# A two-layer window-attention and clustering network on one core: other TensorE work between scores and flips, and three unread products at each strip's end

## The chip, the cores and the metric

One Trainium2 chip, one core. The metric is the time of one execution on the device in microseconds (us): the median over runs. Three runs of the kernel before gave 10057.81, 10078.72 and 10090.93 us.

## What is computed

The input is x, 2 x 96 x 256 x 256 in fp32; the output has its shape. Two layers follow one another, each a mixing part and a feed-forward network.

Layer 0 is cut into four 128 x 128 quadrants per image (8 in all). In a quadrant, with a halo of 2, windows of 8 x 8 queries attend to 12 x 12 keys, with 6 heads of 16 and a relative position term:

```
xn   = (x - mean_c) * rsqrt(var_c + 1e-6)
S    = q k^T + rel_w + rel_h          # 64 x 144 per window and head
x1   = x + proj(softmax(S) v)
x2   = x1 + W2 relu(W1 q(ln(x1)) + b1) + b2    # fp8 weights and operands, fp16 sums
```

Layer 1 pools features of a quadrant into 4 centres per head (4 heads of 24), gives every point to its nearest centre by cosine similarity (the winner alone, with a sigmoid weight), gathers the points' values by centre, and mixes them back to the points: `xc = x2 + proj(sim * agg)`. Its feed-forward network is like that of layer 0.

## The kernel before

**Tiling.** The 8 quadrants have 16 strips of 8 rows each, N = 128 strips. A strip is 32 windows, 16 to the left and 16 to the right in parity, worked on as TILES = 8 pairs p; a pair fills 128 partitions with 2 windows of 64 queries.

**Stages.** Strips run as a software pipeline. In step n, `attend` does the attention of strip n, the preparation of strip n + 1 (mean, variance, normalisation, keys, queries, values: `ahead`), the feed-forward network of strip n - 1 (`b1`), pooling of n - 2 (`b2`), from step 18 on (LAG_B) the features and similarities of the quadrant before (`on.b`), from step 34 on (LAG_C) mixing and the second feed-forward network (`on.c1`, `c2`, `c3`). This gives three stages: steps 0 to 17, 18 to 33, 34 to 127. Behind them, 34 `drain` steps finish layer 1 for the last quadrants. Between quadrants, `edge` works out the centres.

**Order of the work.** Each engine has its own program, written out by hand; a Signal is a semaphore with a count per step, and `at(n, k)` is the value at which the k-th of step n is done. The order in a program is thus the order on the engine: nothing is reordered by a planner. PE's program is written out for 16 strips in a loop over quadrants; DVE's loop body in stage 3 holds two strips.

**A strip on PE** (`attend`, L624 to 841). scores(0); flip_z(0) of strip n - 1; make_values(1); then for each p: scores(p+1) into both banks of `scores_x` (L627, waits until DVE has shifted pair p), flip(p, 0) and flip(p, 1) (L646, transposes of the shifted scores into `flipped`, wait for the shift of p), weigh(p-1) (L669, probabilities times values, waits for the exponentials of p - 1), and then other work, which differs by p: mean, flip_z(1), output_c at 0; mean, flip_features, hidden at 1; hidden, variance, features at 2; hidden, variance, flip_zc, make_values(2) at 3; make_values(3), flip_sims and output at 4; pool, flip_heads, spread, hidden_c at 5; project, spread, hidden_c at 6; hidden_c and mix at 7. The tail (L816 to 841) is make_keys 0 and 1, weigh(7), then make_queries 0 to 5 with make_keys 2 and 3, flip_heads(1), make_main, project(1) and make_rest between them, and gather.

**PSUM.** Eight banks: `work` (bank0, bank1) for mean, spread, values, queries, features, flip_zc and mix; `scores_x` (two) for scores, and at the strip's end for make_keys, whose results ACT stores (k_stored); `flipped` (two) for the flips, hidden layers, outputs and the first values; `pv`; and `misc` for small transposes and projections.

**A strip on DVE** (L1468 to 1576). For each p: maximum of the scores (L1496), two subtractions (L1500, L1504), and then other work: stats_c (L1729) and rsqrt_c (L1740, nine small operations in a row, each waiting for the one before) at p = 0; centre_x at 1 and 2; output_c at 1; hidden (L1611, bias and relu of layer 0) at 2, 3, 4; normalise_c (L1748) at 2; compare at 3; variance, a Newton step and lengths at 4; normalise(0) (L1471) and cosine at 5; normalise_x, output, hidden_c at 6 and 7. Then mix (L1722), next_stats (L1626), normalise(1), ffn_stats, pool_stats, ffn_normalise(0), hidden_c, best_of (L1688), residual(1), ffn_stats, ffn_normalise(1), and add_gathered (L1716, waits for PE's gather). The next strip's first maximum follows.

**A strip on ACT** (L1133 to 1230). For each p: two exponentials (L1147, L1150), then evacuations, squares and quantisations for the work that PE has done in that pair; in the tail, the stores of keys (L1107), queries (L1113) and values.

**POOL** masks values, gathers windows and normalises the stream; **SP** issues all transfers. Neither program changes.

```
def make_keys(n, c):
    ...
    mm(score[c % 2][0:C, 0:CH], wk[0:PROW, :], xn_flat[0:PROW, c * CH:(c + 1) * CH],
       start=True, stop=True).then_inc(k_ready.sem, 1)
```

Here CH is 396, a quarter of a strip's 1584 columns.

## Time and profile before

| | |
|---|---|
| median of three runs | 10078.72 us (10057.81 to 10090.93) |
| the profiled execution | 10158.83 us, its span 10157.0 us |
| mean granted TensorE clock | 0.860 |
| PE busy | 9070.3 us (89%), 177778 instructions |
| PE weight loads busy | 7381.3 us (73%) |
| DVE busy | 7288.7 us (72%), 24125 |
| ACT busy | 5171.8 us (51%), 10122 |
| POOL busy | 2170.7 us (21%), 4356 |
| DMA | 509 MB, 50 GB/s in the mean |

A busy PE is not a PE at its peak: the time of a matmul in the profile includes its passage through the array, and at the lower clock the same instruction takes about twice as long. The granted clock is therefore read beside every busy share. What a wait costs is read from the chain of waits and from the timeline of the stage, for an engine that waits off the chain loses nothing. The names in the rows are those of tensors without buffer numbers: `flipped` stands for both of its banks, `bank` for `work`, `later` for the buffers of layer 1 (xc, xn2b, xn2_t, feat_sq), `rz` for rs_c_chain, `z` for z8, `h` for h16 and h8.

### The profile page before, as it was taken

How to read it: one execution, taken by the hardware profiler on the slowest of the kernel's cores; microseconds unless marked ns; L12 is line 12 of the kernel's file. 1: busy time of each engine (PE TensorE's matmuls, PEld its weight loads, DVE VectorE, ACT ScalarE, POOL GpSimd, SP SyncE). 2: the span in 40 equal slices, each digit the busy share in tenths (PEclk: the TensorE clock that was granted, in tenths of full speed). 3: DMA queues.
4: the chain of work that ended last, by engine and by line, in shares of the span. 5: the costliest groups of instructions: out<-in, count | busy, mean ns of one | idle time of the engine just before them, and what ended most of it. 6: DMA issues, size and time to landing. Idle time of an engine off the chain costs nothing.

```text
span 10157.0 us, 445903 instructions
## 1 busy us (share of the span) xinstructions
PE 9070.3 (89%) x177778; PEld 7381.3 (73%) x177778; DVE 7288.7 (72%) x24125; ACT 5171.8 (51%) x10122; POOL 2170.7 (21%) x4356
## 2 busy tenths in 40 slices
PE   8999999999998999989999999989989999997666
PEld 6777778777777777777777777777777777776554
DVE  5777777777777777777777777777777777776555
ACT  4555444445555555555555555555555555554445
POOL 2333222222222222222222222222222222221000
PEclk9999998998898888888888888888888888897555
DMA  2111111112121211212111111112112112121111
GB/s 60 44 47 45 48 48 48 48 51 51 51 54 50 55 50 50 55 49 51 51 51 50 50 52 50 50 50 55 51 50 55 47 50 53 52 53 44 43 45 47
DMA packets 191702, 509.43 MB, mean 50 GB/s; under 512 B 33214, under 2 KB 66686, under 8 KB 189694
## 3 DMA queue, kind: packets, MB, share of 16 engines
q1 hardware_dynamic: 189918, 482.96, 17.9%
q8 instruction: 1447, 23.71, 1.0%
q14 instruction: 337, 2.76, 0.1%
HBM read 244.54 MB, written 160.43 MB: 40 GB/s over the span
## 4 chain that ended last, share of the span: by engine, by line
PE 70%; DVE 18%; issue 7%; ACT 4%; DVEq 0%; SPq 0%; ACTq 0%; DMA 0%; POOL 0%; POOLq 0%
PE scores_x L639 9%; PE flipped L661 8%; PE scores_x L580 4%; PE pv L689 4%; PE bank L609 4%; PE bank L546 3%; PE misc L555 3%; PE bank L927 3%; PE bank L598 3%; PE pv L683 3%; PE bank L900 3%; PE bank L616 2%; PE pv L883 2%; DVE maxes L1496 2%; PE misc L718 2%
## 5 line engine op out<-in xcount | busy, mean ns | idle before, releaser
L1931 POOL TENSOR_TENSOR vrest<-vstage,vmask 96x384 f32<-96x384 f32 x512 | 432.0, 844 | 5560.4 <-ACT vstage L1125 5560.2
L1496 DVE TENSOR_REDUCE maxes<-scores_x 128x6 f32<-128x864 f32 x1024 | 1078.2, 1053 | 573.3 <-PE scores_x L639 465.6
L639 PE MATMUL scores_x<-keys,queries 64*64 64x144 f32 x24576 | 1171.5, 328 | 297.2 <-DVE shifted L1504 283.2
L639 PEld LDWEIGHTS scores_x<-keys,queries 64*64 64x64 f32 x24576 | 855.2, 152 | 457.4 <-issue 408.1
L1147 ACT ACTIVATE probs<-flipped 128x384 f32<-128x384 f32 x1024 | 501.4, 490 | 1314.2 <-PE flipped L661 1313.7
L661 PE MATMUL flipped<-ident,shifted 128*128 128x128 f32 x6144 | 1034.5, 310 | 61.5 <-ACT h16c L1298 46.5
L661 PEld LDWEIGHTS flipped<-ident,shifted 128*128 128x128 f32 x6144 | 750.0, 156 | 346.9 <-issue 222.8
L601 PE MATMUL bank<-xn,wq 97*32 97x64 f32 x24576 | 946.8, 233 | 59.4 <-issue 59.0
L1504 DVE TENSOR_TENSOR shifted<-scores_x,maxes 128x768 f32<-128x768 f32 x1024 | 969.8, 947 | 0.2 <-issue 0.2
L598 PEld LDWEIGHTS bank<-xt,wq 97*32 97x32 f32 x24576 | 806.2, 119 | 205.1 <-issue 179.9
L598 PE MATMUL bank<-xt,wq 97*32 97x64 f32 x24576 | 929.0, 234 | 29.0 <-issue 27.8
L1113 ACT ACTIVATE queries<-bank 128x512 f32<-128x512 f32 x768 | 458.6, 597 | 835.4 <-PE bank L601 835.4
L601 PEld LDWEIGHTS bank<-xn,wq 97*32 97x32 f32 x24576 | 821.5, 117 | 43.0 <-issue 42.4
L1944 POOL TENSOR_SCALAR xn<-x,mr 128x96 f32<-128x96 f32 x1024 | 690.3, 686 | 42.3 <-DVE mr L1404 42.3
L689 PE MATMUL pv<-vmain,probs 128*32 128x17 f32 x49152 | 643.6, 189 | 3.5 <-issue 3.5
L689 PEld LDWEIGHTS pv<-vmain,probs 128*32 128x32 f32 x49152 | 638.6, 116 | 2.5 <-issue 2.4
L1150 ACT ACTIVATE probs<-flipped 128x512 f32<-128x512 f32 x1024 | 611.0, 597 | 55.5 <-PE flipped L664 54.4
L1904 POOL COPY xt<-xn 97x512 f32<-97x512 f32 x256 | 291.0, 1167 | 1493.2 <-DVE xn L1464 1493.2
L1613 DVE TENSOR_SCALAR h<-h,b1q 128x512 f16<-128x512 f16 x768 | 261.8, 351 | 450.4 <-ACT h L1240 409.6
L609 PE MATMUL bank<-wv,win_xn 97*128 97x96 f32 x3072 | 497.0, 313 | 96.3 <-ACT z8ct L1293 96.1
L580 PE MATMUL scores_x<-xn,wk 97*96 97x396 f32 x1024 | 564.4, 665 | 1.1 <-DVE xn L1464 0.7
L1298 ACT ACTIVATE h16c<-flipped 128x512 f16<-128x512 f32 x768 | 421.4, 591 | 281.2 <-PE flipped L945 281.2
(180 smaller groups left out, 19648.2 us busy)
## 6 DMA issues: line engine op xcount, KB each, us to landing
x_in<-x_dram SPq DMA_DIRECT2D x128, 594.0 KB
keys<-kst SPq DMA_DIRECT2D x768, 99.0 KB
xn_kept<-xn SPq DMA_DIRECT2D x128, 388.0 KB, 3.9
later<-xn_kept SPq DMA_DIRECT2D x128, 388.0 KB, 3.4
x_tok<-tok_dram SPq DMA_DIRECT2D x128, 384.0 KB, 3.5
x_kept<-x SPq DMA_DIRECT2D x128, 384.0 KB, 2.4
later<-x_kept SPq DMA_DIRECT2D x128, 384.0 KB, 4.7
out_dram<-later SPq DMA_DIRECT2D x128, 384.0 KB, 2.3
```

The costliest lines, as they stand in the source:

```text
L580: mm(score[c % 2][0:C, 0:CH], wk[0:PROW, :], xn_flat[0:PROW, c * CH:(c + 1) * CH], start=True, stop=True).then_inc(k_ready.sem, 1)
L598: mm(dst[64 * e:64 * e + 32, :, :, j], wq[0:PROW, p * WS + j, 2 * g + e, :], xt[0:PROW, p, j, :, :], start=True, stop=True, skip_group_che ...
L601: last = mm(dst[64 * e + 32:64 * e + 64, :, j, :], wq[0:PROW, 2 * WS + j, 2 * g + e, :], rows[:, j], start=True, stop=True, skip_group_che ...
L609: last = mm(dst[0][:, j * C:(j + 1) * C], win_xn[:, 4 * i + j, 0:MAIN], wv[0:PROW, :], start=True, stop=True)
L639: last = mm(score[e][64 * j:64 * j + 64, g * NKEY:(g + 1) * NKEY], queries[64 * e:64 * e + 64, g, w, :], keys[64 * e:64 * e + 64, g, :, WS ...
L661: last = nc.tensor.transpose(flipped[:, e, g * 128:(g + 1) * 128], shifted[:, p % 2, e * NG + g, :], ident[:, :])
L689: last = mm(pv[tok_, at + i * VC:at + (i + 1) * VC], probs[:, p % 2, i, tok_], vmain[:, 2 * p + part // 2, i, :], start=False, stop=True, ...
L1147: run(probs[:, p % 2, 0:NG, :].rearrange("p i n -> p (i n)"), flipped[:, 0, 0:NG * 128], ACT.Exp).then_inc(exp_ready.sem, 1)
L1150: run(probs[:, p % 2, NG:NH + 1, :].rearrange("p i n -> p (i n)"), flipped[:, 1, :], ACT.Exp).then_inc(exp_ready.sem, 1)
L1496: V.tensor_reduce(maxes[:, p % 2, :, :], sc, AX.X, ALU.max).then_inc(max_ready.sem, 1)
L1504: V.tensor_tensor(shifted[:, p % 2, :, :].rearrange("p (e g) k -> p e g k", e=2), sc[:, :, :, 0:MAIN], maxes[:, p % 2, :, :, None].to_broa ...
L1944: last = P.tensor_scalar(xn2[:, t, 0:C], x2[:, t, :], mr[:, t, 0:1], mr[:, t, 1:2], ALU.subtract, ALU.mult)
```

## The change

PE's program: in each pair, part of the other work is now done between scores(p+1) and the flips of p, and part of it goes to another pair. keep_busy is new: three products with the operands of make_keys into the score banks, with no signal; nothing reads what they write. mix goes from p = 7 to behind weigh(7). ACT's program follows PE's order. DVE's: rsqrt_c goes from p = 0 to 1, output_c from 1 to 2, normalise_c from 2 to 3, hidden from 2, 3, 4 to 3, 4, 5, normalise(0) behind cosine, normalise_x(0), (1) from 6 to 7, hidden_c from 6 and 7 to 7 alone. The first hunks of the diff are the PE program with its new function, the others ACT's and DVE's; lines with only "..." leave out unchanged or removed code.

```diff
@@ -580,6 +580,12 @@
+            def keep_busy(n, i):
+
+                pe.wait_ge(k_stored.sem, k_stored.at(n, 4))
+                mm(score[i % 2][0:C, 0:CH], wk[0:PROW, :], xn_flat[0:PROW, i * CH:(i + 1) * CH],
+                   start=True, stop=True)
+
@@ -726,97 +732,106 @@
                 for p in range(TILES):
                     if p + 1 < TILES:
                         scores(p + 1)
+                    if p == 0 and ahead:
+                        pe.wait_ge(v_stored.sem, v_stored.at(n, 4))
+                        mean(n + 1, 0)
+                        mean(n + 1, 1)
+                    if p == 1 and ahead:
+                        mean(n + 1, 2)
+                        mean(n + 1, 3)
+                    if p == 2 and on.b:
+                        for u in range(2):
+                            if ahead:
+                                pe.wait_ge(centred.sem, centred.at(n + 1, 3 + u))
+                            pe.wait_ge(v_stored.sem, v_stored.at(n, 4))
+                            features(n, u)
+                    if p == 3 and ahead:
+                        variance(n + 1, 2, on)
+                        variance(n + 1, 3, on)
+                    if p == 4:
+                        pe.wait_ge(v_stored.sem, v_stored.at(n, 4))
+                        if ahead:
+                            pe.wait_ge(centred.sem, centred.at(n + 1, 4))
+                        if on.c2:
+                            pe.wait_ge(zct_ready.sem, zct_ready.at(n, 2))
+                        elif on.b:
+                            pe.wait_ge(fsq_ready.sem, fsq_ready.at(n, 2))
+                            pe.wait_ge(dots_ready.sem, dots_ready.at(n, 2))
+                        make_values(n, 2, work)
+                    if p == 5:
+                        pe.wait_ge(v_stored.sem, v_stored.at(n, 6))
+                        make_values(n, 3, work)
+                    if p == 6:
+                        if ahead:
+                            spread(n + 1, 0)
+                            spread(n + 1, 1)
+                        flip_heads(0)
+                    if p == 7:
+                        if ahead:
+                            spread(n + 1, 2)
+                            spread(n + 1, 3)
+                        project(0)
                     flip(p, 0)
                     flip(p, 1)
                     if p >= 1:
                         weigh(p - 1)
                     if p == 0:
...
                         if b1:
                             flip_z(n - 1, 1)
                         if on.c3:
                             pe.wait_ge(exp_ready.sem, exp_ready.at(n, 2))
                             output_c(n, 0)
                             output_c(n, 1)
...
+                    if p == 1 and on.b:
+                        if b1:
+                            pe.wait_ge(zt_ready.sem, zt_ready.at(n - 1, 2))
+                        flip_features(n, 0, k % 2)
+                    if p == 2 and ahead:
+                        if b1:
+                            pe.wait_ge(zt_ready.sem, zt_ready.at(n - 1, 2))
+                        variance(n + 1, 0, on)
+                        variance(n + 1, 1, on)
+                    if p == 3 and on.c2:
+                        pe.wait_ge(fsq_ready.sem, fsq_ready.at(n, 2))
+                        pe.wait_ge(dots_ready.sem, dots_ready.at(n, 2))
+                        flip_zc(n, 0)
+                        flip_zc(n, 1)
+                    if p == 4 and on.c1:
                         if ahead:
...
+                            pe.wait_ge(newton_x.sem, newton_x.at(n + 1, 1))
+                        flip_sims(n, 0, on)
+                    if p == 5:
+                        if b2:
+                            pool(n - 2)
+                        if on.c1:
+                            flip_sims(n, 1, on)
                     if b1 and p in (1, 2, 3):
                         pe.wait_ge(exp_ready.sem, exp_ready.at(n, 2 * p + 2))
                         hidden(n - 1, 2 * p - 2)
                         hidden(n - 1, 2 * p - 1)
                     if p == 1 and on.b:
                         flip_features(n, 1, k % 2)
...
+                    if b1 and p == 4:
+                        pe.wait_ge(exp_ready.sem, exp_ready.at(n, 10))
+                        output(n - 1, 0)
+                        output(n - 1, 1)
                     if on.c2 and p in (5, 6, 7):
                         pe.wait_ge(exp_ready.sem, exp_ready.at(n, 2 * p + 2))
                         hidden_c(n, 2 * p - 10)
                         hidden_c(n, 2 * p - 9)
...
                 if ahead:
                     make_keys(n + 1, 0)
                     make_keys(n + 1, 1)
                 weigh(TILES - 1)
+                if on.c1:
+                    for u in range(2):
+                        if ahead:
+                            pe.wait_ge(normed.sem, normed.at(n + 1, 4 - u))
+                        pe.wait_ge(v_stored.sem, v_stored.at(n, 8))
+                        mix(n, u)
                 if ahead:
                     make_queries(n + 1, 0, on)
                     make_keys(n + 1, 2)
@@ -829,13 +844,16 @@
                         pe.wait_ge(hc_evac.sem, hc_evac.at(n, 5))
                     make_main(n + 1, 0, fill)
                     make_queries(n + 1, 3)
+                    keep_busy(n + 1, 0)
                 project(1)
                 if ahead:
                     make_queries(n + 1, 4)
+                    keep_busy(n + 1, 1)
                     make_queries(n + 1, 5)
                     if on.c2:
                         pe.wait_ge(hc_evac.sem, hc_evac.at(n, 6))
                     make_rest(n + 1, 0, fill)
+                    keep_busy(n + 1, 2)
                 if on.b:
                     pe.wait_ge(heads_ready.sem, heads_ready.at(n, 2))
                     gather(n, k % 2)
@@ -1141,6 +1159,22 @@
+                    if p == 1 and ahead:
+                        square(n + 1, 0)
+                        square(n + 1, 1)
+                    if p == 2:
+                        if ahead:
+                            square(n + 1, 2)
+                            square(n + 1, 3)
+                        if on.b:
+                            square_features(n, 0)
+                            square_features(n, 1)
+                    if p == 4:
+                        store_values(n, 2, work)
+                    if p == 5:
+                        store_values(n, 3, work)
+                    if p == 6:
+                        heads(0)
@@ -1156,9 +1190,6 @@
-                        if ahead:
-                            square(n + 1, 0)
-                            square(n + 1, 1)
@@ -1166,18 +1197,11 @@
-                    if p == 2:
-                        if b1:
-                            hidden(n - 1, 2)
-                            hidden(n - 1, 3)
-                            quantise(n - 1, 0)
-                            quantise(n - 1, 1)
-                        if ahead:
-                            square(n + 1, 2)
-                            square(n + 1, 3)
-                        if on.b:
-                            square_features(n, 0)
-                            square_features(n, 1)
+                    if p == 2 and b1:
+                        hidden(n - 1, 2)
+                        hidden(n - 1, 3)
+                        quantise(n - 1, 0)
+                        quantise(n - 1, 1)
@@ -1187,21 +1211,16 @@
-                        store_values(n, 2, work)
+                        if on.c1:
+                            store_sims(n, 0)
-                        store_values(n, 3, work)
-                        if on.c1:
-                            store_sims(n, 0)
-                        if b1:
-                        if on.c1:
-                            store_sims(n, 1)
-                    if p == 5:
-                        heads(0)
+                    if p == 5 and on.c1:
+                        store_sims(n, 1)
@@ -1507,21 +1526,23 @@
-                        rsqrt_c(n)
-                    if p == 1 and on.c3:
+                    if p == 1 and on.c2:
+                        rsqrt_c(n)
+                    if b1 and p in (3, 4, 5):
+                        hidden(n - 1, 2 * p - 6)
+                        hidden(n - 1, 2 * p - 5)
+                    if p == 2 and on.c3:
-                    if b1 and p in (2, 3, 4):
-                        hidden(n - 1, 2 * p - 4)
-                        hidden(n - 1, 2 * p - 3)
-                    if p == 2 and on.c2:
-                        normalise_c(n, 1 - par)
-                    if p == 3 and on.b:
-                        compare(n, 0)
-                        compare(n, 1)
+                    if p == 3:
+                        if on.b:
+                            compare(n, 0)
+                            compare(n, 1)
+                        if on.c2:
+                            normalise_c(n, 1 - par)
@@ -1533,13 +1554,10 @@
-                        normalise(0)
+                        normalise(0)
-                        if ahead:
-                            normalise_x(n + 1, 0)
-                            normalise_x(n + 1, 1)
@@ -1548,12 +1566,18 @@
+                            normalise_x(n + 1, 0)
+                            normalise_x(n + 1, 1)
+                        if on.c2:
+                            hidden_c(n, 0)
+                            hidden_c(n, 1)
+                        if ahead:
-                    if on.c2 and p in (6, 7):
-                        hidden_c(n, 2 * p - 12)
-                        hidden_c(n, 2 * p - 11)
+                        if on.c2:
+                            hidden_c(n, 2)
+                            hidden_c(n, 3)
```

## Rows read from the trace of the kernel before

**Rows 1.** The page: granted TensorE clock in 40 slices; the chain's shares by engine.

```profile
PEclk9999998998898888888888888888888888897555
...
PE 70%; DVE 18%; issue 7%; ACT 4%; DVEq 0%; SPq 0%; ACTq 0%; DMA 0%; POOL 0%; POOLq 0%
```

**Rows 2.** Windows by stage: us, busy us of each engine (instructions), granted clock, DMA share, GB/s.

```profile
74.00:1075.00 1001.00, 947.48 (x23085) 780.16 (x23084) 707.21 (x2127) 513.14 (x993) 298.73 (x606) 0.98 0.18 46
1075.00:2101.00 1026.00, 973.61 (x21232) 814.26 (x21233) 744.31 (x2292) 499.88 (x976) 270.39 (x545) 0.91 0.19 48
2101.00:9297.00 7196.00, 6554.08 (x130040) 5347.04 (x130041) 5341.34 (x17620) 3761.60 (x7407) 1588.80 (x3174) 0.88 0.20 51
```

**Rows 3.** Waits of PE in stage 3: who waited for whom: us in total, times, longest.

```profile
PE scores_x L639 <- DVE shifted L1504: 261.4, 119, 5.7
PE bank L609 <- ACT z8ct L1293: 96.1, 93, 1.1
PE flipped L945 <- ACT probs L1150: 90.1, 93, 1.0
PE flipped L661 <- ACT h16c L1298: 46.5, 93, 0.6
```

**Rows 4.** Windows of one strip of stage 3, cut where the granted clock changes.

```profile
7095.60:7099.10 3.50, 0.43 (x14) 0.45 (x17) 3.33 (x10) 0.54 (x2) 0.00 (x0) 1.00 0.15 54
7099.10:7102.50 3.40, 3.40 (x71) 2.66 (x66) 3.20 (x8) 1.21 (x3) 0.00 (x0) 0.50 0.06 23
...
7119.60:7123.00 3.40, 3.40 (x35) 2.84 (x35) 3.06 (x14) 1.79 (x4) 0.84 (x1) 0.50 0.00 0
...
7143.50:7150.30 6.80, 6.80 (x128) 4.70 (x130) 3.53 (x15) 1.77 (x4) 3.60 (x14) 0.50 0.01 2
```

**Rows 5.** Timeline of DVE, the same strip: start, us, line, what, idle before.

```profile
7093.11 0.18 DVE L1742 TENSOR_SCALAR rz<-mv_z 128x8 f32<-128x8 f32 x1
...
7093.56 1.65 DVE L1387 TENSOR_TENSOR rz<-rz 128x8 f32<-128x8 f32 x1
...
7096.33 1.05 DVE L1496 TENSOR_REDUCE maxes<-scores_x 128x6 f32<-128x864 f32 x1
...
7119.04 0.84 DVE L1613 TENSOR_SCALAR h<-h,b1q 128x512 f16<-128x512 f16 x2 [2.98 <-ACT h L1240]
...
7122.80 1.05 DVE L1496 TENSOR_REDUCE maxes<-scores_x 128x6 f32<-128x864 f32 x1
```

**Rows 6.** Chain of waits, the same strip: start, us on the chain, engine and line.

```profile
7098.69 1.37 PE scores_x L639 x24
...
7120.99 1.65 PE scores_x L639 x24
...
7124.46 1.06 PE bank L609 x8
...
7128.10 0.90 PE scores_x L639 x24
...
7142.34 2.59 PE bank L927 x16
7144.93 2.88 PE scores_x L580 x4
...
7150.56 0.84 PE scores_x L580 x2
```

**Rows 7.** Timeline of ACT, the same strip.

```profile
7124.27 1.14 ACT L1246 ACTIVATE h<-h 128x512 fp8e5<-128x512 f16 x2
```

**Rows 8.** Timeline of DVE, end of this strip and start of the next.

```profile
7149.13 0.16 DVE L1475 COPY pool_parts<-pv 97x2 f32 x1 [2.32 <-PE pv L689]
...
7166.33 0.17 DVE L1719 TENSOR_TENSOR gathered<-gathered,pv 97x16 f32<-97x16 f32 x1 [2.76 <-PE pv L908]
7169.41 1.06 DVE L1496 TENSOR_REDUCE maxes<-scores_x 128x6 f32<-128x864 f32 x1 [2.91 <-issue]
```

**Rows 9.** Window of PE's transposes and one-column products in the same strip.

```profile
7130.60:7133.70 3.10, 3.10 (x38) 2.68 (x37) 1.50 (x3) 0.69 (x2) 0.00 (x0) 1.00 0.28 106
```

More of the change, by code:

```diff
@@ L781, in attend @@
-                    if p == 4:
-                        pe.wait_ge(v_stored.sem, v_stored.at(n, 6))
-                        make_values(n, 3, work)
-                        if on.c1:
-                            if ahead:
-                                pe.wait_ge(newton_x.sem, newton_x.at(n + 1, 1))
-                            flip_sims(n, 0, on)
-                        if b1:
-                            pe.wait_ge(exp_ready.sem, exp_ready.at(n, 10))
-                            output(n - 1, 0)
-                            output(n - 1, 1)
-                        if on.c1:
-                            flip_sims(n, 1, on)
@@ L809, in attend @@
                         hidden_c(n, 2 * p - 9)
-                    if p == 7 and on.c1:
-                        for u in range(2):
-                            if ahead:
-                                pe.wait_ge(normed.sem, normed.at(n + 1, 4 - u))
-                            pe.wait_ge(v_stored.sem, v_stored.at(n, 8))
-                            mix(n, u)
                 if ahead:
@@ L1158, in attend @@
                     if p == 1:
-                        if ahead:
-                            square(n + 1, 0)
-                            square(n + 1, 1)
                         if on.b:
```

48 lines of the change are left out of this document (removed).

## The prediction

> **What bounds the kernel now.** I read the page first. The granted clock of TensorE is what to see there: it stands near 1 in the first eighth and at 0.8 to 0.9 in nearly all that follows, and PE carries 70% of the chain that ended last [rows 1]. Then the windows by stage. Stage 3 (strips 34 to 127, all three layers in flight) takes 7196 us for 94 strips, 76.6 us each, at a clock of 0.88 with PE busy 91%; stage 1 (strips 0 to 17) takes 55.6 each at 0.98 and stage 2 (18 to 33) 64.1 each at 0.91 [rows 2]. The drains behind them run code that the change doesn't touch. So stage 3 decides.
>
> There PE's own waits come next: 261 us in 94 strips for scores that wait for DVE's shift (2.8 per strip), 1.0 for z8ct, 1.0 for the exponentials ahead of the last hidden product, 0.5 for h16c [rows 3]. In the windows of one strip the clock stands beside them: PE is nearly idle for 3.5 us and the clock is at its lower level (1.2 of 2.4 GHz) in the 3.4 us that follow; it is low again for 3.4 us behind the z8ct wait and for 6.8 us behind the one for the exponentials [rows 4]. PE is the bound from the third group of scores to the last weighing; around the strip's end the bound is DVE.
>
> The first wait has its cause on DVE: between the shifts of pairs 0 and 1 it does stats_c and then rsqrt_c, nine small operations from 7093.11 to 7096.33, one of which took 1.65 us here instead of about 0.18 [rows 5].
>
> **The change, part by part.** I cut a strip in two, with T the start of scores(2).
>
> *T to normalise(1).* In this strip T is 7098.69 [rows 6] and normalise(1) (L1475) starts at 7149.13 [rows 8]: 50.4 us. PE has the same instructions afterwards, in another order.
> 1. make_values(2) moves from behind flip_zc to the next pair. Between flip_zc and the zct_ready wait now stand two hidden products and scores(5), 1.5 us, against ACT's two stores of 1.1: the wait of 1.0 goes.
> 2. spread(2), spread(3) and project(0) move ahead of flips(7), with which the h16c wait (0.5) is covered. The wait for exp(7) stays: ACT still does its hidden_c, similarity and quantise_c first. I take 0.5 of its 1.0 as gone.
> 3. A new wait at output(n-1, 1). It needs quantise(5), so DVE's hidden(5), which moves from pair 4 to pair 5, behind DVE's maximum and shift. DVE's list of pair 4 takes 3.8 us (from hidden at 7119.04 to the next maximum at 7122.80 [rows 5]), and puts that maximum some 1.9 us behind the start of scores(5). Then 2.3 for maximum and shift, 0.6 for hidden, 1.1 for ACT's two quantise [rows 7], with a store of sims ahead of them: 6.0 to 6.4 us. PE does values, both flips of sims and both outputs in the 3.6 us from 7124.46 to 7128.10 [rows 6], of which 1.0 falls to the second sims and output; with 0.9 for scores and 1.6 for flips and weighing at full clock it is there after 5.1. Wait: **+1.2** (0.5 to 2).
> 4. rsqrt_c moves to pair 1 behind centre_x, where PE has mean, flips, weigh, feature flips and hidden before it wants shift(2): 5.5 us against DVE's 2.3 + 1.0 + 2.3. No wait. normalise_c moves to pair 3 behind compare; flip_zc comes 4.4 us after scores(4), as late as DVE has it: 0 (up to +0.5).
> 5. squares, square_features, store_values and heads move ahead of the exponentials on ACT. Their products stand ahead of the flips on PE too, so an exponential waits only for what PE has done before; the longest is square_features, 1.1 us, behind which weigh(1) and variance (2 us) cover the exponentials that hidden(2) waits for: 0.
> 6. mix moves behind make_keys(0), (1) and weigh(7). For PE the sum is the same. For DVE it is not: mixing (0.6 behind the last product) and next_stats (1.4) used to fill its idle 2.3 us ahead of normalise(1) [rows 8] and now stand between weigh(7) and normalise(1): **+1.9**.
> 7. Clock. The 3.4 us behind z8ct and the 6.8 behind exp(7) [rows 4] cost about half of themselves: scores 1.65 against 0.90, two keys 2.88 against 0.84 for one [rows 6]; together 1.4 + 2.1. The first cause goes; the second is halved. But the new wait of step 3 stands between thin work (weigh, flip_sims) and can lower the clock as those do. I take -1.4 - 1.0 + 1.0 = **-1.4**. The 3.4 us behind T's own wait (1.4) go to the next stretch.
>
> Sum: -1.0 - 1.0 + 1.2 + 1.9 - 1.4 - 1.4 = **-1.7**.
>
> *normalise(1) to T, 26.2 us in the mean (76.6 - 50.4).* DVE needs 17.2 us to L1719 here, of which it waits 2.8 for PE's gather; then 2.9 us of issue ahead of the first maximum, at the end of a loop body that holds two strips [rows 8].
> 8. keep_busy: one product is 0.84 us at full clock, 1.44 at half [rows 6], so 2.5 to 4.3 us of TensorE per strip. The score banks are idle there (no keys to store, scores(0) not yet due), and the wait on k_stored(4) has long been met. What hides them in stage 3 is DVE: normalise(1), two normalisations, best_of, residual(1) go on without PE. If weigh(7) ends at 0, DVE's scores(1) permit comes at 4.0 (mix, mixing, next_stats) + 16.2 (17.2 - 2.8, and to the maximum 3.1 where the loop turns, 0.5 elsewhere, 1.8 in the mean) + 2.4 (shift) = 22.6. PE's scores(0) was done 18 us after weigh(7) in this strip, whose tail was half cold; plus mix 2.0, plus products 2.5 of which some 1 stands in waits for ACT's stores, plus flip_z and values 1.9: 23.4. Cover is about equal to cost: **0**, up to +2.0 where the tail is cold, and a gain where the products keep the clock up.
> 9. The gather's 2.8 come in one strip of two at most and PE's slack takes part: **-0.5**.
> 10. scores(2)'s own wait, 3.07 in this strip, small in the next, is gone with rsqrt_c: I take half of the 1.8 that it is in the mean, and all of what the clock loses behind it (1.4 in this strip) goes to the idle at scores(1), which is there now. **-0.9**, and 0 for the clock.
>
> Sum: **-1.4** with step 9; and the 1.4 of T's clock counted above is given back by half, **+0.7**, since a later T follows a stretch at low clock.
>
> Stage 3: -1.7 - 1.4 + 0.7 = -2.4, with 0.4 for mean strips, whose clock lies lower than this one's in its first half: **-2.8 per strip**, 94 strips: -263 us. Bounds: from +2.5 to -6.
>
> *Stages 1 and 2.* In stage 1 PE is busy 95% at full clock [rows 2]: nothing hides the products there, 2.5 us, but ACT's stores of queries let PE wait about 1.0 of it; project ahead of flips(7) saves 0.4; output(1) waits 0.5 longer: **+1.3** x 18 = +23 (bounds 0 and +55). Stage 2 has both the clock's loss and no mix: **-1.0** x 16 = -16 (bounds -50 to +40).
>
> **Sum.** -263 + 23 - 16 = -256. The profiled execution took 10158.8 us around its span of 10157.0, 80 more than the median of the runs (10078.7). 10158.8 - 256 = 9903 profiled, 9823 in the median; I say 9820.
>
> **Rivals.**
> *A, slower:* the mixing that now stands between weigh(7) and normalise(1). If the clock in T to normalise(1) stays as it is, and each low stretch there (such as that behind the new wait at output(1)) lasts 6.8 us instead of 3.4, steps 1 and 2 give 2.0, while steps 3, 6 and that clock cost 1.2 + 1.9 + 3.4 = 6.5 and the tail gives 1.4: +3.1, less 0.6 for what PE's slack takes up. +2.5 x 94 = +235: 10310. It decides as soon as T to normalise(1) lasts over 53 us. Against it: two of three causes of low clock lose their wait. Chance 0.15.
> *B, no change:* what PE saves is waited for at scores(1), for DVE's chain across the strip's end is the bound: 10060 to 10100. For it: DVE was behind PE there already; chance 0.08. A weaker form, -0.4 to -1.4 per strip, 9950 to 10040: 0.10.
> *C, the clock stays up:* the three products carry it over the strip's end and no low stretch is left from T on: another 2 to 3 us per strip, 9550 to 9620. Against it: PE still idles for DVE at scores(1). Chance 0.10.
> *D, transposes:* in pair 6 spread, flip_heads and flips(6) now follow one another, 2.1 us of transposes only, and if these didn't count as work the clock would fall there: 1.7 us per strip more, 9980. Before, flip_heads and spread stand behind the one-column products of pool, and the window of these has the clock at 1.00 [rows 9], so little speaks for it: 0.04.
> By the Trainium skill (TensorE: Matmul & The Clock Gate, Part 4, PE-mode transpose) transposes do not count as TensorE being busy for its clock gate; by that rule D would be the forecast. The trace does not bear it out in that window.
> *E:* the products do not do what they say. They have no reader and no signal, so nothing could wait for them; the only thing they can do is take TensorE's time and hold its clock. That is in C and step 8.
>
> **Chances and range.** The forecast (-1.5 to -4.5 per strip): 0.53. With C, D and the weak form of B that is 0.77 faster; 0.08 within 0.3% (30 us, about what a measurement of this kernel can tell from none), 0.15 slower. The range, 9610 to 10110, takes in the forecast with its bounds, B, D and the weak form, and leaves out A and half of C.
>
> **What would show it.** Right: no wait ahead of values(2) and flips(7); one of about 1.2 us ahead of output(n-1, 1); rsqrt_c behind centre_x; T to normalise(1) at 46 to 49 us; a clock in stage 3 of 0.90 to 0.93; stage 1 longer by some 20 us. Wrong: T to normalise(1) over 50, a clock at or under 0.88, DVE never waiting for scores(0), or PE's gather ending behind DVE's z8 in most strips, by which the three products would be on the path.

## The result, and the profile after

The changed kernel takes 10014.57 us, the kernel before 10077.87 (medians of 20 runs each, 9955.49 to 10090.45 and 10023.01 to 10122.23): a ratio of 0.9945, 95% interval 0.9923 to 0.9968. It is faster by 63 us. The forecast was 9820, faster by 256: the direction was right, three quarters of the gain did not come. The profiled execution lies 32 under its median (9983.0, span 9981.1), that of before 81 over its own, so the two profiles differ by 176 where the medians differ by 63; per-strip gains read from them are too large by about 1 us in all. Of the runs below, one of six with quantise first took 9959.1 us and one of six of the best version 11346.8 at a granted clock of 0.673; without them the two medians are 14 and 0.1 us lower.

The page of the changed kernel, granted clock and shares of the chain (before: [rows 1]):

```profile
PEclk9999999999888989989999898999988899886555
...
PE 74%; DVE 13%; issue 6%; ACT 5%; DVEq 0%; SPq 0%; ACTq 0%; POOL 0%; DMA 0%; POOLq 0%
```

TensorE has more of the chain (74 against 70%), DVE less (13 against 18%). Windows by stage of the changed kernel, columns as in [rows 2]:

```profile
73.00:1092.00 1019.00, 988.85 (x23199) 790.29 (x23198) 718.71 (x2127) 501.06 (x994) 298.42 (x606) 0.97 0.18 45
1092.00:2085.00 993.00, 958.67 (x21324) 778.92 (x21324) 738.67 (x2292) 490.71 (x976) 270.62 (x545) 0.97 0.19 49
2085.00:9123.00 7038.00, 6573.49 (x130614) 5305.42 (x130615) 5306.26 (x17626) 3692.22 (x7408) 1591.32 (x3174) 0.90 0.20 52
```

Against [rows 2] a strip takes 56.6 us instead of 55.6 in stage 1, 62.1 instead of 64.1 in stage 2, 74.9 instead of 76.6 in stage 3. PE's waits in stage 3 (before: [rows 3]):

```profile
PE scores_x L645 <- DVE shifted L1523: 166.8, 77, 5.3
PE flipped L892 <- ACT h L1265: 121.8, 94, 1.3
PE flipped L971 <- ACT probs L1184: 46.9, 92, 0.7
PE flipped L963 <- ACT probs L1184: 25.8, 93, 0.9
```

The waits for z8ct (96 us) and h16c (46) are gone, that for the exponentials fell from 90 to 26 at hidden_c (L963), the one for the shift from 261 to 167. Two waits are new: L892 is output(n-1, 1), 1.3 us in every strip, and L971 is output_c, which now waits 0.5 us per strip for the exponentials (0.6 us in all of stage 3 before). So what PE waits for exponentials in all went only from 90 to 73 us.

Where the rest went is seen by cutting each strip in three. The means below are taken over strips 36 to 125 of a trace without 49, 65, 81, 97 and 113, one in each block of 16, which have a length of their own: 85 strips. T is the start of scores(2), N the start of DVE's normalise(1), M the first maximum of the next strip; "low" is the time of the strip at a granted clock of 0.50, in brackets that in T to N.

| kernel | strip | T to N | N to M | low |
|---|---|---|---|---|
| before | 76.4 | 49.4 | 17.6 | 18.5 (10.4) |
| changed | 74.5 | 46.2 | 19.4 | 14.4 (3.0) |

T to N came out well: 3.2 us shorter, and TensorE's clock is low there for 3.0 us instead of 10.4. N to M is 1.8 us longer where I had said shorter. It is not longer in every strip. In 37 of the 85 the clock is up for at least 10 us behind N and N to M takes 17.35 us, in 32 it is low for a part of them and it takes 18.0; in **16 strips the whole tail runs at the lower clock and N to M takes 27.15**. These 16 alone are (27.15 - 17.35) x 16 / 85 = 1.8 us per strip in the mean. In strips 36 to 125 the clock stays low for over 30 us at a time 17 times (up to 44.4); before it never did (23.9 at most). All 17 stretches begin 1.9 to 3.8 us behind the start of mix, and PE idles for at most 0.33 us in the 8 us ahead of each.

Strip 62 is one of them. Its windows, cut where the clock changes (columns as in [rows 2]):

```profile
4183.40:4232.30 48.90, 46.81 (x938) 38.65 (x934) 34.80 (x90) 29.82 (x62) 9.05 (x22) 0.93 0.17 49
4232.30:4269.90 37.60, 37.25 (x473) 29.00 (x472) 21.82 (x103) 9.92 (x19) 7.92 (x12) 0.50 0.18 41
4269.90:4290.00 20.10, 19.74 (x385) 16.07 (x383) 16.42 (x45) 13.56 (x28) 0.00 (x0) 1.00 0.25 72
```

PE is busy for 37.25 of 37.6 us, at half clock. Its timeline in the changed kernel, from the first keys to the first unread product (L586):

```profile
4226.41 1.49 PE L580 MATMUL scores_x<-xn,wk 97*96 97x396 f32 x4
4227.83 0.38 PE L689 MATMUL pv<-vrest,probs 96*32 96x102 f32 x8
4228.03 0.60 PE L695 MATMUL pv<-vmain,probs 128*32 128x17 f32 x48
4228.56 2.02 PE L945 MATMUL bank<-mix_w,simw_t 17*128 17x96 f32 x16
...
4234.65 1.64 PE L580 MATMUL scores_x<-xn,wk 97*96 97x396 f32 x2
...
4242.75 1.64 PE L586 MATMUL scores_x<-xn,wk 97*96 97x396 f32 x2
```

and DVE's, same strip:

```profile
4229.84 0.56 DVE L1749 TENSOR_TENSOR later<-later,bank 128x384 f32<-128x384 f32 x1 [3.16 <-PE bank L945]
4231.09 1.37 DVE L1653 BATCH_NORM_STATS2 bn_c<-x 128x6 f32<-128x96 f32 x8
4232.38 0.14 DVE L1494 COPY pool_parts<-pv 97x2 f32 x1
4246.08 0.55 DVE L1508 TENSOR_TENSOR x<-x_tok,misc 128x384 f32<-128x384 f32 x1 [4.03 <-PE misc L724]
...
4256.69 0.17 DVE L1743 TENSOR_TENSOR gathered<-gathered,pv 97x16 f32<-97x16 f32 x1 [5.73 <-PE pv L926]
4258.37 1.06 DVE L1515 TENSOR_REDUCE maxes<-scores_x 128x6 f32<-128x864 f32 x1 [1.51 <-PE scores_x L645]
```

Two things are to be seen. DVE idles 3.16 for mix, then mixes, does next_stats, and reaches normalise(1) 3.8 us behind the end of weigh(7) (3.75 in the mean of the 85 strips, 0.18 in the kernel before). And with the clock low, DVE waits for PE three more times: 4.0 for project(1), 5.7 for the gather, 1.5 for scores(0). In such a strip PE is last, and the unread products stand in its way.

### The profile page after: what moved, and what is told of

It is laid out like the page before. It is cut to its first block, busy times and chain, and to the rows that moved or that the text cites. A ratio compares the mean times of both kernels' runs of the same rounds, so it can differ in the third digit from the quotient of the medians.

```text
span 9981.1 us, 447427 instructions
## 1 busy us (share of the span) xinstructions
PE 9114.3 (91%) x178540; PEld 7312.0 (73%) x178540; DVE 7257.7 (73%) x24125; ACT 5080.8 (51%) x10122; POOL 2173.1 (22%) x4356
## 4 chain that ended last, share of the span: by engine, by line
PE 74%; DVE 13%; issue 6%; ACT 5%; DVEq 0%; SPq 0%; ACTq 0%; POOL 0%; DMA 0%; POOLq 0%
PE scores_x L645 10%; PE bank L604 6%; PE flipped L667 6%; PE scores_x L580 4%; PE bank L546 4%; PE misc L555 4%; PE pv L695 3%; PE bank L945 3%; PE bank L615 3%; PE bank L918 3%; PE scores_x L586 3%; DVE maxes L1515 3%; PE pv L689 2%; PE bank L607 2%; PE bank L622 2%
## 5 line engine op out<-in xcount | busy, mean ns | idle before, releaser
L645 PE MATMUL scores_x<-keys,queries 64*64 64x144 f32 x24576 | 1059.7, 306 | 188.0 <-DVE shifted L1523 183.1
L645 PEld LDWEIGHTS scores_x<-keys,queries 64*64 64x64 f32 x24576 | 772.7, 141 | 419.8 <-issue 380.3
L604 PEld LDWEIGHTS bank<-xt,wq 97*32 97x32 f32 x24576 | 843.9, 123 | 269.9 <-issue 160.7
L607 PE MATMUL bank<-xn,wq 97*32 97x64 f32 x24576 | 1003.1, 240 | 9.1 <-issue 8.7
L604 PE MATMUL bank<-xt,wq 97*32 97x64 f32 x24576 | 985.2, 240 | 9.9 <-issue 6.5
L667 PE MATMUL flipped<-ident,shifted 128*128 128x128 f32 x6144 | 898.9, 285 | 0.0
L607 PEld LDWEIGHTS bank<-xn,wq 97*32 97x32 f32 x24576 | 857.3, 121 | 12.3 <-issue 12.0
L1259 ACT ACTIVATE h<-flipped 128x512 f16<-128x512 f32 x768 | 415.7, 595 | 266.0 <-PE flipped L882 266.0
L1937 POOL COPY win_xn<-xn 97x144 f32<-97x144 f32 x2048 | 539.4, 310 | 0.0
L580 PE MATMUL scores_x<-xn,wk 97*96 97x396 f32 x1024 | 498.9, 593 | 1.1 <-DVE xn L1483 0.7
```

Source lines behind the costliest of these rows:

```text
L604: mm(dst[64 * e:64 * e + 32, :, :, j], wq[0:PROW, p * WS + j, 2 * g + e, :], xt[0:PROW, p, j, :, :], start=True, stop=True, skip_group_che ...
L607: last = mm(dst[64 * e + 32:64 * e + 64, :, j, :], wq[0:PROW, 2 * WS + j, 2 * g + e, :], rows[:, j], start=True, stop=True, skip_group_che ...
L645: last = mm(score[e][64 * j:64 * j + 64, g * NKEY:(g + 1) * NKEY], queries[64 * e:64 * e + 64, g, w, :], keys[64 * e:64 * e + 64, g, :, WS ...
L667: last = nc.tensor.transpose(flipped[:, e, g * 128:(g + 1) * 128], shifted[:, p % 2, e * NG + g, :], ident[:, :])
L1937: last = P.tensor_copy(win_xn[:, w, :].rearrange("p (a b) -> p a b", b=KW), xn[0:PROW, :, WS * w:WS * w + KW])
```

## The experiments

Each median is set against the kernel before, run beside it; the ratio's 95% interval is in brackets. "Changed" is the changed kernel's median, 10014.6. It was not measured beside the experiments, and the medians of the kernel before vary by 17 us between their groups of runs, so a difference from "changed" of under some 50 us is weak; the 2x2 comparison below holds by medians and by ratios alike.

**The products.** First the changed kernel without them.

```diff
-                    keep_busy(n + 1, 0)
-                    keep_busy(n + 1, 1)
-                    keep_busy(n + 1, 2)
```

> The changed kernel without its three unread products. Theory P (the products lie on the path: PE's tail is as long as DVE's, so what I put at zero in step 8 costs): stage 1 gets 1.0 to 1.2 us per strip shorter (back to 55.6), stage 3 by 1 to 2 us per strip, the whole 9850 to 9930 against 10015 for the changed kernel; in the profile DVE no longer waits for PE's gather ahead of add_gathered (1.25 us in the mean now). Theory K (the products hold the granted clock up at the strip's end, and pay for themselves): the clock in stage 3 falls under 0.90, and the whole is 10015 or above, up to 10150.

9875.5, 0.9777 [0.9749, 0.9804]: the products cost 139 us. Its profile shows less than half of that, for it is that of the slowest of the five runs (9928.7). In it stage 1 takes 55.5 us per strip instead of 56.6, but that is within what profiles of other orders scatter by (with mix ahead 56.0, with the products or without), so no loss in stage 1 is shown. In stage 3 the first 10 us behind N are low in 27 strips instead of 16. In 10 of these the tail is low to its end and takes 23.8 us, 3.3 less than 27.15; in the other 17 the clock comes back after some 16 us, which it does in no such strip of the changed kernel. Over all 85, N to M is 0.9 shorter in the mean (18.5). So the products keep some tails from starting low, and lengthen those that do.

Then the products alone, in the kernel before.

```diff
                     make_queries(n + 1, 3)
+                    keep_busy(n + 1, 0)
...
                     make_queries(n + 1, 4)
+                    keep_busy(n + 1, 1)
...
                     make_rest(n + 1, 0, fill)
+                    keep_busy(n + 1, 2)
```

> The kernel before with the three unread products and nothing else of the change. Theory P: +1 us per strip in stages 1 and 2, +1 to +2 in stage 3, 10150 to 10300 against 10078. Theory K: the clock of stage 3 rises over 0.90 and the whole is at 10000 to 10078.

10087.3, 0.9994 [0.9976, 1.0013]: nothing. Time at low clock falls from 18.5 to 12.9 us per strip and no stretch lasts over 17.1; N to M stays 17.5. A window over most of its stage 3 (columns as in [rows 2]):

```profile
2085.00:8700.00 6615.00, 6066.12 (x120938) 4884.81 (x120928) 4963.27 (x16300) 3472.85 (x6832) 1476.20 (x2953) 0.91 0.20 51
```

N to M shows neither a cost nor a gain with 2.5 us less at low clock in it, as one expects where DVE is the bound at the strip's end and the products lie in PE's slack. That a cost and a gain by the clock cancel is not excluded by this run.

**The place of mix.** mix goes back to pair 7 in the changed kernel.

```diff
+                    if p == 7 and on.c1:
+                        for u in range(2):
...
+                            mix(n, u)
                 if ahead:
                     make_keys(n + 1, 0)
                     make_keys(n + 1, 1)
                 weigh(TILES - 1)
-                if on.c1:
-                    for u in range(2):
...
-                        mix(n, u)
```

> The changed kernel with mix back in pair 7, ahead of make_keys. If step 6 is right (mixing and next_stats between weigh(7) and normalise(1) lengthen DVE's chain over the strip's end) and DVE is the bound there: 1 to 2 us per strip of stage 3 shorter, 9830 to 9920. Rival (PE is the bound in the tail, with its low clock behind the thin products of mix): within 30 us of 10015, normalise(1) earlier but scores(1) not.

9677.6, 0.9598 [0.9572, 0.9624]: 337 us faster than changed, far more than the step 6 theory's 9830 to 9920; its rival (no gain) is refuted. DVE's timeline of this kernel in one strip of the same part:

```profile
4046.62 1.37 DVE L1653 BATCH_NORM_STATS2 bn_c<-x 128x6 f32<-128x96 f32 x8
4050.09 0.16 DVE L1494 COPY pool_parts<-pv 97x2 f32 x1 [2.10 <-PE pv L695]
...
4067.91 1.06 DVE L1515 TENSOR_REDUCE maxes<-scores_x 128x6 f32<-128x864 f32 x1 [2.50 <-issue]
```

Mixing and next_stats lie ahead of DVE's wait for weigh(7) again. A window over most of stage 3:

```profile
2085.00:8730.00 6645.00, 6242.38 (x129401) 5037.40 (x129397) 5243.58 (x17415) 3659.04 (x7312) 1572.56 (x3150) 0.94 0.21 55
```

N to M is 17.4, 2.0 less than in the changed kernel, and T to N 45.4, 0.8 less: most of the gain lies behind N. In no strip is the tail low throughout; in 6 it is low for 8.5 to 9.4 us, and N to M is 20.4 there.

The same without the products (both edits above):

> The changed kernel with mix back in pair 7 and without the three products (both edits of e1 and e3, which gave 139 and 337 us). If the products are simply PE's time on the path in the tail, the two add: 9530 to 9580. If instead, as in the kernel before, they now lie under DVE's chain (e3's profile has DVE, not PE, last at the strip's end), they cost nothing with mix ahead, or even pay by the clock: 9660 to 9720.

9727.6, 0.9648 [0.9619, 0.9676]: 50 slower than with them. With mix ahead the products pay; with mix behind they cost 139. The four kernels side by side, medians and ratios to the kernel before:

| | with products | without |
|---|---|---|
| mix behind weigh(7) | 10014.6 (0.9945) | 9875.5 (0.9777) |
| mix in pair 7 | 9677.6 (0.9598) | 9727.6 (0.9648) |

mix's place costs 337 us with the products and 148 without. mix alone moved late, in the kernel before:

> The kernel before with mix alone moved behind weigh(7). By e3 the move costs 3.4 us per strip of stage 3 in the changed kernel. If that is DVE's chain (mixing and next_stats between weigh(7) and normalise(1)), it costs here as well: 10250 to 10400. If it is the low clock through PE's tail that follows mix there, the low stretch that the kernel before has behind the wait for the exponentials is moved too and the cost is smaller, 10080 to 10200.

10153.0, 1.0081 [1.0055, 1.0106]: some 75 us dearer (69 by the medians, 82 by the ratio), not 337. So mix's late place costs something in each kernel (75, 148, 337), and by far the most where the products stand behind it. The low clock behind N rises here too, from 4.0 to 7.2 us per strip, with 4 stretches of 30.7 us, though there are no products. Next, changed with the order keys(0), (1), mix, weigh(7):

```diff
-                weigh(TILES - 1)
                 if on.c1:
                     for u in range(2):
...
                         mix(n, u)
+                weigh(TILES - 1)
```

> The changed kernel with mix between make_keys(1) and weigh(7) instead of behind weigh(7): DVE gets mix 0.7 us earlier, and PE's thin products (mix, weigh) stay side by side in the other order, with the queries behind them. Theory DVE (lateness of mixing is the cost): about a third of e3's gain, 9880 to 9930. Theory clock (keys, the dense products, must stand between mix and the end so that the tail does not start at the low clock): 9980 to 10040, and the share of strips whose whole tail is at the low clock stays near one in five.

9799.0, 0.9742 [0.9705, 0.9779]: 216 faster than changed. That is two thirds of the 337, and outside both expectations. The same thin products stand side by side, with the same queries behind them, and yet only 3 stretches last over 30 us instead of 17 in its profile (that of the fastest of six runs, 9699.3, so the count is low for it too): thin work with nothing dense behind it does not seem enough to make the tail stay low.

**DVE's lateness alone.** In the changed kernel, DVE's normalise(1) ahead of mixing and next_stats; PE's order stays.

```diff
+                normalise(1)
                 if on.c1:
                     mix(n, 0, par)
                     mix(n, 1, par)
                 if b1:
                     next_stats(n - 1)
-                normalise(1)
```

> The changed kernel with DVE's order alone turned: normalise(1) ahead of mixing and next_stats, PE's order untouched (mix behind weigh(7)). If my step 6 (DVE's 1.9 us between weigh(7) and normalise(1)) is what mix's new place costs, most of e3's 337 us comes back: 9700 to 9800. If it is PE's low clock behind mix, normalise(1) starts 2.5 to 3.5 us earlier but the long stretches at the low clock stay (10 to 20) and the whole stays at 9960 to 10050.

9809.5, 0.9729 [0.9702, 0.9756]: 205 faster than changed. N comes 4.0 earlier (T to N 42.2) and N to M is 2.6 longer, for mixing and next_stats are in it now. The stretches over 30 us are still there, 12 of them. So DVE's order alone is worth 205 us with PE's order as it is. That the other 130 or so of the 337 are the low tail's is not shown: this edit brings N forward by 4.0 where mix ahead brings it by 0.8, and effects do not add in this kernel (see Open).

**What makes the tail stay low.** One product between mix(1) and make_queries(0), dense work behind the thin (its last argument is the count of stored keys that it waits for):

```diff
                         mix(n, u)
+                if ahead:
+                    keep_busy(n + 1, 0, 1)
...
-                    keep_busy(n + 1, 0)
```

> The changed kernel with the first of its three products moved up: it stands between mix(1) and make_queries(0) now (into bank 0, once ACT has stored keys(1)). In the changed kernel's profile 17 stretches of 31 to 44 us at the low clock begin behind mix. Theory thin work (mix on 17 rows, then queries in 32 columns, with nothing dense between): one dense product between them makes those long stretches rarer, 9800 to 9920. Theory DVE (mix stands too late for DVE's chain, whatever PE does): the same median as the changed kernel within 40 us of 10015, and as many long stretches.

9911.2, 0.9838 [0.98, 0.9875]: 103 faster than changed's 10014.6; 7 stretches over 30 us instead of 17. All three earlier, behind make_keys(3), flip_heads(1) and make_queries(2):

> The changed kernel with its three products moved to the first half of the tail: behind make_keys(3), behind flip_heads(1) and behind make_queries(2). Theory thin work: the clock comes back sooner where it fell behind mix, fewer long stretches at the low clock, 9850 to 9960. Theory P (they cost their time wherever they stand in the tail): within 40 us of 10015.

9973.0, 0.9888 [0.9864, 0.9912]: no stretch over 30 us is left, but in 45 of 85 strips N to M has 8 to 12 us at low clock, and stage 1 takes 57.8 per strip. The median is 42 under changed's: the long stretches can be had away by placing dense work, and what takes their place costs nearly as much. The changed kernel once more, one run beside these two:

> The changed kernel once more, for a second profile: 10 to 20 stretches of over 30 us at the low clock in stage 3 if they are a habit of this order and not of one execution; T to normalise(1) 46 us again.

9936.8, with 11 stretches over 30 us instead of 17 and the same 46.3 for T to N: a count from one trace varies by that much between executions, and six stretches at 9.8 us are 59 us. This one run is also 19 us under the lowest of changed's 20, and beside it the two experiments differ from changed by -26 and +36 us: neither the 103 nor the 42 is safe. The count of 7 with the product behind mix is weak evidence, the count of none with all three early lies well outside 11 to 17.

**The wait at output(n-1, 1).** I had put it on DVE's hidden(5). DVE's hidden back to pairs 2, 3, 4:

```diff
-                    if b1 and p in (3, 4, 5):
-                        hidden(n - 1, 2 * p - 6)
-                        hidden(n - 1, 2 * p - 5)
+                    if b1 and p in (2, 3, 4):
+                        hidden(n - 1, 2 * p - 4)
+                        hidden(n - 1, 2 * p - 3)
```

> The changed kernel with DVE's hidden (bias and relu) back in pairs 2, 3, 4 instead of 3, 4, 5. Step 3 says that PE's wait inside output(n-1, 1), 1.5 us in the changed kernel's profile, comes from that alone: output(0) and output(1) together last 1.2 instead of 2.6 us. If T to normalise(1) counts in full: -1.4 us per strip of all 110 strips of stages 2 and 3, 9850 to 9900. Rival (what PE saves here it waits for at scores(1), DVE being the bound over the strip's end): within 40 us of 10015.

10177.9, 1.008 [1.0056, 1.0104]: 163 slower than changed, where both expectations had it no slower than 40. PE's waits in this kernel:

```profile
PE scores_x L645 <- DVE shifted L1523: 245.4, 154, 5.1
PE flipped L892 <- ACT h L1265: 121.9, 94, 1.3
```

The wait is the same to 0.1 us, so DVE's hidden isn't its cause. DVE now waits for its hidden's input again (354 us in stage 3, 5 in the changed kernel, 350 in the kernel before), and PE for DVE's shift (154 times instead of 77). Then ACT's list, with mix ahead: quantise(4), (5) before store_sims(0).

```diff
                     if p == 4:
-                        if on.c1:
-                            store_sims(n, 0)
                         if b1:
                             quantise(n - 1, 4)
                             quantise(n - 1, 5)
+                        if on.c1:
+                            store_sims(n, 0)
+                        if b1:
                             output(n - 1, 0)
```

> e3 (the changed kernel with mix back in pair 7) with ACT's quantise(4), (5) ahead of store_sims(0). e4 left the wait inside output(n-1, 1) at 1.3 us per strip, so it isn't DVE's hidden that sets it but ACT's list behind the exponentials. Expected: that wait falls by 0.6 us (the store of sims) per strip, 94 strips: 9600 to 9640 against e3's 9678. Rival: PE waits for the same time at scores(1): 9660 to 9700.

9572.0, 0.9489 [0.9463, 0.9515]: 106 faster than mix ahead alone. L892 is gone from PE's waits:

```profile
PE scores_x L645 <- DVE shifted L1524: 130.8, 91, 3.0
PE flipped L971 <- ACT probs L1184: 48.5, 92, 0.7
```

store_sims (L1305) waits for PE's flip_sims and holds the two quantise (L1265) behind it. ACT's and PE's timelines in strip 62 of the changed kernel:

```profile
4209.34 0.59 ACT L1305 ACTIVATE simw_t<-misc 17x512 f32<-17x512 f32 x1 [0.73 <-PE misc L938]
4209.84 1.13 ACT L1265 ACTIVATE h<-h 128x512 fp8e5<-128x512 f16 x2
...
4211.11 0.67 PE L892 MATMUL flipped<-w2q,h 128*128 128x96 fp8e5 x12 [1.29 <-ACT h L1265]
```

The store takes 0.59 and waits 0.73 before it; only the 0.59 was in the expectation, which the gain exceeds. The same edit with mix late:

> The changed kernel, mix where the change puts it, with ACT's quantise(4), (5) ahead of store_sims(0). It took 106 us off e3. If T to normalise(1) counts in full in the changed kernel too: 9900 to 9930. If what is saved there is lost in the tail (PE's low clock): 9960 to 10020.

9804.7, 0.9738 [0.9706, 0.9771]: 210 faster than changed, twice as much as with mix ahead and beyond both expectations. 8 long stretches are left; less low clock upstream of the tail is one reading of that, which nothing here tests.

**rsqrt_c alone**, in the kernel before: from pair 0 to behind centre_x of pair 1.

```diff
                         stats_c(n, 1 - par)
-                        rsqrt_c(n)
...
+                    if p == 1 and on.c2:
+                        rsqrt_c(n)
```

> The kernel before with rsqrt_c alone moved from pair 0 to pair 1 on DVE. If scores(2)'s wait is DVE's chain as step 10 says: T (start of scores(2)) about 0.9 us earlier in the strip in the mean, -0.5 to -1.3 us per strip of stage 3, 9960 to 10030, with less low clock behind it. Rival (PE had as much else to do): within 20 us of 10080.

9989.3, 0.9922 [0.9898, 0.9947]: 95 us faster, more than the whole change. PE's wait for the shift falls from 261 to about 180 us, and scores(1) to T from 6.8 to 5.7 us.

**The best version.** e11 with variance(n+1, 2) and (3) behind weigh(2) instead of ahead of flips(3), so that weighing parts the one-column products.

```diff
-                    if p == 3 and ahead:
-                        variance(n + 1, 2, on)
-                        variance(n + 1, 3, on)
...
+                    if p == 3 and ahead:
+                        variance(n + 1, 2, on)
+                        variance(n + 1, 3, on)
                     if p == 3 and on.c2:
```

> e11 with variance(2), (3) behind weigh(2), not ahead of flips(3), so that the two groups of one-column products stand 2.6 us apart instead of 1.4. e11's low clock in T to normalise(1) (4.5 us per strip) lies behind them. Theory: it gets rarer, 9520 to 9560. Rival (DVE gets its variance later and the pair behind it waits, or the products are as thin in either place): 9560 to 9620.

9477.1, 0.9406 [0.938, 0.9432]: 95 faster than e11, more than expected, and 5.4% faster than the changed kernel. The low clock in T to N falls from 4.5 to 1.7 us per strip. A window over most of stage 3:

```profile
2085.00:8540.00 6455.00, 6116.49 (x128987) 4930.38 (x128986) 5223.73 (x17410) 3628.37 (x7289) 1574.92 (x3158) 0.96 0.22 56
```

## Why the prediction was right in its sign and wrong in its size

**Right.** Steps 1 and 2: both waits went, and the one for the exponentials at hidden_c fell to 0.3 per strip where I left 0.5; but output_c now waits 0.5 for them, which no step had. Steps 4 and 10: rsqrt_c, -95 us when moved alone; I had 0.9 per strip, 85 us. T to N at 46.2, forecast 46 to 49. Stage 1: +1.0 per strip, forecast +1.3 (+0.5 in the changed kernel's second profile); stage 2: -2.0, forecast -1.0. The clock of stage 3 at 0.90, the lower end of 0.90 to 0.93.

**Step 7 was too small a gain:** T to N fell by 3.2, not 1.7. (The forecast took 50.4 us of one strip for it; the mean was 49.4.) Its low clock fell by 7.4 us per strip, where I had taken 1.4 us of time, i.e. some 3 us of low clock.

**Step 3: right size, wrong cause.** 1.3 us measured, 1.2 forecast. My chain led over DVE's hidden(5); e4 moved it and the wait stayed. It is ACT's store_sims(0) ahead of the quantises (e11). The row of ACT's quantise was read, the list it stands in was not: store_sims itself waits for PE.

**Step 8 failed.** It held that the three products' cover is about equal to their cost and put them at 0, "up to +2.0 where the tail is cold". Measured: 139 us of the 193 that are missing (e1); 0 in the kernel before (e2) and a gain of 50 with mix ahead (e5). Without them the change would have given 202 us of the 256. Its comparison was of PE and DVE at scores(1), and left out that DVE's first maximum waits for scores(0). By its own figures the maximum came 4.0 + 16.2 = 20.2 us behind weigh(7), and scores(0) was done at 18 + 2.0 + 1.5 = 21.5: PE was already last. The profiles have, in the mean of the 85 strips, the end of scores(0) 16.1 us behind the end of weigh(7) before and 21.5 after, and the first maximum at 17.8 and 23.2. And it took a tail half cold at worst: the clock is low all through it in 16 strips of 85, where N to M takes 9.8 us more than where it is up. The expected -1.4 + 0.7 of N to T became +1.3 in these profiles (28.3 us less 27.0).

**Step 6: right size, one term missing.** N stands 3.6 us later behind weigh(7) than before; less mix's 2.0 of PE's time, that is 1.6 per strip, forecast 1.9. It had no term for PE's side: with mix behind weigh(7) the clock often falls there and, in the changed kernel, can stay down over the whole tail. The sum in time shows it: 179 us forecast for mix's place, 148 measured without the products, 337 with them. How the remaining 54 of the 193 divide over the steps is not known.

**The rivals.** A had its finger on the right place (mixing between weigh(7) and normalise(1)) but on the wrong stretch: the low clock came behind N, not in T to N. C came only half: the products do hold the clock up in some strips, at a price in the others. D did not come: the window of [rows 9] had the clock at 1.00, and in pairs 6 and 7 of the changed kernel, where spread, flip_heads and flips now follow one another, it stays at 1.00 too: from scores(6) to the first keys it is low in none of the 85 strips (in 53 of them before). Window of strip 62 of the changed kernel, from pair 5 to weigh(7) and beyond (columns as in [rows 2]):

```profile
4212.00:4232.30 20.30, 19.82 (x449) 16.45 (x441) 13.64 (x29) 11.85 (x25) 8.21 (x21) 1.00 0.16 46
```

The rule of the Trainium skill (TensorE: Matmul & The Clock Gate, Part 4, PE-mode transpose) that transposes don't count for the clock gate is not borne out by either window, though neither has more than about 2 us of transposes in a row.

**Open.** Why the clock stays down through the tail in one strip of five and not in the others. That it begins behind mix, with PE busy, is shown; thin work alone explains it badly, since mix between the keys and weigh(7) leaves 3 of the 17 stretches and ACT's order alone leaves 8 (one profile each). Their number also differs from execution to execution. Nor do the effects add: mix late costs 75 in the kernel before, 148 in the changed one without products and 337 with them; quantise first is worth 106 with mix ahead and 210 without.

## What to carry to other kernels

A filler is free only while its engine isn't last: before adding one, look at the worst clock state its place can see, not the mean, and price it there. Work that an engine used to do while it waited (here DVE's mixing and next_stats ahead of weigh(7)) costs up to its full time once it stands behind that wait; keep the late engine's own work ahead of the event that it waits for. When a wait is traced to an engine, read the whole list ahead of the releasing instruction there, and test the cause by moving one item before building on it.

## What the runs showed of the hardware

The granted clock stays at 0.50 for as long as 41 us while PE is hardly ever idle (0.6 us of the 41; busy 37.25 of 37.6 us in strip 62's window; in the longest stretch, 44.4 us, PE idles for 7.3). That surprised me; I had tied every low stretch to a wait just ahead of it. Here the products ahead of it are the 17-column and 17-row ones of weigh and mix and, in most cases, the first queries of 64 columns; that these are the reason is not shown. In the same strip two keys products (four records) take 1.49 us at full clock and one (two records) 1.64 at low. And a clock that is better in the mean need not be worth anything: the products alone raise it from 0.88 to about 0.91 in stage 3, and the time stays the same to 0.2%.
